# Reordering the first projections, running the first feed-forward in split passes, and moving the last layer's row sums to VectorE

## The reference, cut to what matters

```python
# layer 0, attention: 32 heads of 128, 4 key/value heads, keys from [context, latents]
q = (latents @ Wq).reshape(b, q_len, 4, 8, 128)
k = (hidden_states @ Wk).reshape(b, kv_len, 4, 128)
v = (hidden_states @ Wv).reshape(b, kv_len, 4, 128)
...
# layer 0, feed-forward: a base product and 8 low-rank experts, mixed by a softmax over the batch mean
base = jnp.einsum('bsi,oi->bso', x, W_org)
q = jnp.einsum('bi,ki->bk', x.mean(axis=1), Wq)
coeffs = jax.nn.softmax(jnp.einsum('bk,ek->be', q, lora_keys) / math.sqrt(K), axis=-1)
h = jnp.einsum('bsi,eir->bser', x, lora_down)
delta = jnp.einsum('be,bser,ero->bso', coeffs, h, lora_up)
return base + delta * (SCALE * MULTIPLIER)
...
# layer 3, attention: a product of two fake-quantised matrices, q1 from the norm, q2 from the context
return jnp.matmul(q1, q2)
```

## Time and profile before

| | |
|---|---|
| median of 3 runs | 1441.21 us (1439.42 to 1441.31) |
| the profiled execution, its own time | 1436.33 us |
| its span | 1433.7 us |
| busy share of the span: PE, PEld, DVE, ACT, POOL | 95%, 75%, 65%, 42%, 33% |
| feed-forward 0, its three products (L867, L874, L911) on PE | 16.2, 14.5 and 13.9 us busy |

### The profile page before, as it was taken

The page is one execution under the profiler, slowest core; times in us unless marked ns, Lnnn a source line. Parts: engine busy times, 40 slices in busy tenths (PEclk is TensorE's granted clock), DMA queues, the critical chain, the costliest instruction groups (busy, mean ns, idle before and its releaser), DMA issues.

```text
span 1433.7 us, 21149 instructions
## 1 busy us (share of the span) xinstructions
PE 1359.5 (95%) x8222; PEld 1080.4 (75%) x8227; DVE 927.7 (65%) x1351; ACT 602.6 (42%) x1046; POOL 473.3 (33%) x361
## 2 busy tenths in 40 slices
PE   4999999999999999989999999999989999799986
PEld 3989889988889889874598888888876444377733
DVE  4488778864588688772457775567665576334278
ACT  2444444443344444430144443344425577323252
POOL 4226436371126426512222653217133000324210
PEclk9999999999999999999999999999999699999999
DMA  5111112121012111102111101002004000263000
GB/s 176 52 39 59 56 40 59 36 70 37 16 53 58 53 52 41 34 1 86 44 38 45 33 29 56 23 18 73 1 1 128 1 2 2 91 159 110 1 0 30
DMA packets 54337, 68.18 MB, mean 48 GB/s; under 512 B 26417, under 2 KB 34897, under 8 KB 54241
## 3 DMA queue, kind: packets, MB, share of 16 engines
q1 hardware_dynamic: 54240, 66.84, 15.5%
HBM read 57.13 MB, written 5.37 MB: 44 GB/s over the span
## 4 chain that ended last, share of the span: by engine, by line
PE 85%; DVE 9%; ACT 3%; issue 1%; DMA 1%; POOL 0%; SPq 0%; DVEq 0%; ACTq 0%; POOLq 0%
PE ps L644 13%; PE ps L619 12%; PE ps L595 9%; PE ps L628 9%; PE ps L588 9%; PE ps L580 5%; PE ps L565 5%; PE ps L1508 4%; PE ps L1129 3%; PE ps L1155 3%; PE ps L1521 2%; PE ps L1111 2%; PE ps L1140 1%; PE ps L867 1%; PE ps L874 1%
## 5 line engine op out<-in xcount | busy, mean ns | idle before, releaser
L713 ACT ACTIVATE pT<-ps 128x768 fp32r<-128x768 f32 x192 | 156.0, 812 | 288.6 <-PE ps L628 287.0
L644 PE MATMUL ps<-pT,vv 128*128 128x256 f32 (+1 forms) x1728 | 251.2, 290 | 2.5 <-DVE oT L823 2.5
L619 PEld LDWEIGHTS ps<-kT,qT 128*128 128x128 f32 (+1 forms) x1152 | 201.5, 188 | 43.9 <-DVE qT L768 3.7
L619 PE MATMUL ps<-kT,qT 128*128 128x512 f32 (+3 forms) x1152 | 231.6, 336 | 2.8 <-DVE qT L768 2.8
L816 DVE TENSOR_TENSOR pT<-ps,pT 128x768 fp32r<-128x768 f32 x192 | 183.7, 957 | 77.8 <-ACT pT L713 77.1
L644 PEld LDWEIGHTS ps<-pT,vv 128*128 128x128 f32 (+1 forms) x1728 | 215.1, 180 | 3.1 <-DVE pT L816 2.9
L721 ACT ACTIVATE prob<-ps,rows_and_turned 128x768 f32<-128x768 f32 x192 | 172.3, 897 | 84.9 <-DVE rows_and_turned L804 84.9
L804 DVE TENSOR_REDUCE rows_and_turned<-ps 128x1 f32<-128x768 f32 x192 | 182.7, 951 | 26.1 <-PE ps L619 25.8
L531 POOL TENSOR_TENSOR wo<-raw,one 128x512 fp32r<-128x512 f32 (+1 forms) x48 | 49.9, 1040 | 394.7 <-PE ps L595 394.3
L595 PE MATMUL ps<-wo,oT 128*128 128x512 f32 (+1 forms) x576 | 169.5, 403 | 5.6 <-DVE qT L768 2.6
L628 PE MATMUL ps<-ident,prob 128*128 128x128 f32 x1152 | 157.1, 272 | 0.4 <-DVE pT L816 0.4
(11 more groups left out here) (236 smaller groups left out, 1890.9 us busy)
## 6 DMA issues: line engine op xcount, KB each, us to landing
f2raw<-in_f_w SPq DMA_DIRECT2D x11, 776.0 KB, 5.0
rows_and_turned<-in_m_w SPq DMA_DIRECT2D x11, 768.0 KB, 4.2
raw<-in_l_wq SPq DMA_DIRECT2D x32, 256.0 KB, 2.7
raw<-in_l_wo SPq DMA_DIRECT2D x32, 256.0 KB, 2.6
raw<-in_l_wq SPq DMA_DIRECT2D x16, 192.0 KB, 2.4
raw<-in_l_wo SPq DMA_DIRECT2D x16, 192.0 KB, 2.4
w3gu<-rows_and_turned SPq DMA_DIRECT2D x11, 256.0 KB, 3.1
ctxraw<-in_ctxT SPq DMA_DIRECT2D x2, 1024.0 KB, 7.4
```

What stands on the lines that cost most here:

```text
L619: last = nc.tensor.matmul(sc[:, lo:hi], qT[0:hd, h % 2, qp, r * P:(r + 1) * P], kT[0:hd, kp, b, lo:hi], start=(qp, kp) == PAIRS[0], stop=( ...
L644: last = nc.tensor.matmul(bank(6, 256, hd), vv[:, vp, b * VT + j, group % 2 * hd:(group % 2 + 1) * hd], pT[:, q % 2, pp, j, :], start=(j = ...
L713: nc.scalar.activation(turned_p(m, HI), ps[:, 4:6, 0:S // 2].rearrange("p a (j c) -> p a j c", j=3), ACT.Copy).then_inc(sem("att_pT_hi"), 1)
```

## The change

Three places change.

1. **The start.** `wk` is loaded before the context. The first context half is split in two parts of two k tiles each, on ACT and DVE, and K job 0 starts on the first. Both parts are split ahead of the norm's statistics, and the second half of the context after the turned rows. POOL computes `rstd` behind the split of `wk`, its first stream entry, and goes on to the next weights with no wait for the context, whose raw copy now lies elsewhere. PE's order is K 0, turns, K 2, Q 0, K 1, and K 1 goes to bank 5.
2. **Feed-forward 0.** All three products run as three split passes. POOL splits `worg` in four pieces during heads 22 to 27 of attention 0. `down` and `up` are loaded when the last scores are done, ACT writes their HI parts when the last weighted sums are, and POOL writes their LO parts (one instruction of 128x2048 each), the first of them only when all four norm rows are written (`rows_ready`). DVE splits the turned rows, in between its norm work, and makes the batch sums in two reductions. The small product with the batch mean comes after the base product, `h` is evicted by ACT (HI) and DVE (LO), and the matmuls that spread the coefficients come directly before the last `down_part`. POOL's first split of attention 1's `wv` waits for the small product.
3. **Attention 3.** DVE writes `rowz` instead of ACT, the row sums of a tile come before the turn of the next, the two small ACT instructions of a row no longer wait for each other, and one add and one clamp on DVE change places.

```diff
         self.first = [("K", 0, 0), ("K", 0, 1), ("K", 0, 2), ("Q", 0, 0)]
+        if before is None:
+            self.first = [("K", 0, 0), ("K", 0, 2), ("Q", 0, 0), ("K", 0, 1)]
...
-            sb("kept0", [P, 12, 512], F32, grp)
+            sb("kept0", [P, 31, 512], F32, grp)
             ctxraw = sb("ctxraw", [P, KT, B * CTX], F32, grp)
...
+        CTX_PARTS = ((0, 0, 2), (0, 2, KT), (1, 0, KT))
...
-                if j == 2:
+                if A is A0 and entry in base_after:
...
+                    nc.gpsimd.tensor_tensor(worg_hi[:, k, :], worg[:, k, :], one[:].to_broadcast([P, D]),
+                                            ALU.mult).then_inc(sem("f0_worg_split"), 1)
...
+                if j == (0 if A is A0 else 2):
                     layer_norm()
...
             if A is A0:
-                pe.wait_ge(sem("ctx_split"), 1)
                 job(A.first[0])
                 turn_pe(pe, u)
-                pe.wait_ge(sem("ctx_split"), 2)
+                pe.wait_ge(sem("xT_lo"), RT)
                 job(A.first[1])
+                job(A.first[2])
+                pe.wait_ge(sem("ctx_split"), 3)
+                job(A.first[3])
...
+                    ln_row_variance(v, s, r, sem("att_w"), A.before["w"] + A.place[what])
+                    if r:
+                        ln_row_out(v, s, r - 1)
+                    if r >= 2:
+                        turn_dve(v, 1, [r - 2], "f0_xT_lo")
+                    if r == RT - 1:
+                        ln_row_out(v, s, r)
...
         def mlp0_sp(sp):
-            sp.wait_ge(sem("layer_done"), 1)
+            att_wait(sp, A0, "scores", A0.items)
...
+        def mlp0_weight_lo(g, dst, raw_weights, n):
+
+            g.wait_ge(sem("f0_w_hi"), n)
+            nc.gpsimd.tensor_tensor(dst[:, LO].rearrange("p k n -> p (k n)"),
+                                    raw_weights[:].rearrange("p k n -> p (k n)"),
+                                    dst[:, HI].bitcast(F32).rearrange("p k n -> p (k n)"),
+                                    ALU.subtract).then_inc(sem("f0_w_lo"), 1)
+
         def mlp0_pool(g):
 
+            g.wait_ge(sem("rows_ready"), RT * 2)
+            mlp0_weight_lo(g, downs, down, 1)
...
             def base(r):
+                pe.wait_ge(sem("f0_xT_lo"), r + 1)
                 for k in range(KT):
-                    nc.tensor.matmul(bank(4 + r), xTf[:, k, r * P:(r + 1) * P], worg[:, k, :],
-                                     start=(k == 0), stop=False)
+                    for xp, wp in PAIRS:
+                        nc.tensor.matmul(bank(4 + r), xT[:, xp, k, r * P:(r + 1) * P],
+                                         (worg_hi, worg_lo)[wp][:, k, :], start=(k == 0 and (xp, wp) == PAIRS[0]),
+                                         stop=False)
...
-            def before_output_weights():
-                ln_first_pool(g)
-                g.wait_ge(sem("ctx_split"), 2)
-
-            att_pool(g, A0, before_output_weights)
+            att_pool(g, A0, lambda: ln_first_pool(g))
...
             split_context(0)
+            split_context(1)
             ln_first_dve(v)
-            split_context(1)
             turn_dve(v, 0)
+            split_context(2)
```

More of the change, by code:

```diff
@@ L425, in turn_act, with turn_dve @@
                                      ACT.Copy).then_inc(sem("xT_hi"), 1)
-        def turn_dve(v, u, which=range(RT)):
+        def turn_dve(v, u, which=range(RT), done="xT_lo"):
             for r in which:
@@ L523, in att_pool @@
                     att_wait(g, A, "w_full", A.place["V", h - 2, 5] if h else 0)
+                    if A is A1 and h == 0 and part == 0:
+                        g.wait_ge(sem("f0_small"), 1)
                 elif w == "q":
@@ L562, in job @@
                     for k in range(KT):
+                        if what == ("K", 0, 0) and A is A0 and k % 2 == 0:
+                            pe.wait_ge(sem("ctx_split"), k // 2 + 1)
                         for wp, xp in PAIRS:
@@ L910, in mlp0_pe @@
                         pe.wait_ge(sem("f0_hT"), (k * B + r // 2) + 1)
-                    last = nc.tensor.matmul(bank(4 + r), hT[:, k, r * P:(r + 1) * P], up[:, k, :],
-                                            start=False, stop=(k == KT - 1))
+                    for hp, wp in PAIRS:
+                        last = nc.tensor.matmul(bank(4 + r), hT[:, hp, k, r * P:(r + 1) * P], ups[:, wp, k, :],
+                                                start=False, stop=(k == KT - 1 and (hp, wp) == PAIRS[-1]))
@@ L913, in mlp0_pe, with mlp0_early_act @@
                 last.then_inc(sem("f0_out"), 1)
+        def mlp0_early_act(a):
+            att_wait(a, A0, "pv", A0.pairs)
+            for dst, raw_weights, name in ((downs, down, "f0_down"), (ups, up, "f0_up")):
+                a.wait_ge(sem(name), 16)
+                nc.scalar.activation(dst[:, HI].rearrange("p k n -> p (k n)"),
+                                     raw_weights[:].rearrange("p k n -> p (k n)"),
+                                     ACT.Copy).then_inc(sem("f0_w_hi"), 1)
         def mlp0_act(a):
@@ new lines, in mlp0_act @@
+            for k in range(KT):
+                a.wait_ge(sem("f0_h"), k + 1)
+                for b in range(B):
+                    nc.scalar.activation(hT[:, HI, k, b * 256:(b + 1) * 256], ps[:, k, b * 256:(b + 1) * 256],
+                                         ACT.Copy, scale=spread[:, k, b:b + 1]).then_inc(sem("f0_hT_hi"), 1)
+        def mlp0_dve(v):
+            for b in range(B):
+                if b == 0:
+                    turn_dve(v, 1, [2], "f0_xT_lo")
+                else:
+                    turn_dve(v, 1, [3], "f0_xT_lo")
+                v.wait_ge(sem("f0_xT_lo"), 2 * b + 2)
+                nc.vector.tensor_reduce(msum[:, :, b], xT[:, :, :, b * 256:(b + 1) * 256].bitcast(F32).rearrange(
+                    "p s k n -> p k s n"), AX.XY, ALU.add).then_inc(sem("f0_msum"), 1)
@@ L1724, in att3_row_act @@
             act_seq.inc(nc.scalar.activation(scale, rstd[:, r:r + 1], ACT.Copy, scale=inv[:, 0:1]))
-            act_seq.wait(a)
-            act_seq.inc(nc.scalar.activation(shift, minus_mean, ACT.Identity, scale=scale, bias=sz[:, 1:2]))
+            act_seq.inc(nc.scalar.activation(shift, minus_mean, ACT.Identity, scale=rstd[:, r:r + 1], bias=sz[:, 1:2]))
             act_seq.wait(a)
```

157 lines of the change are left out of this document (95 added, 62 removed).

## The result

The changed kernel takes 1422.97 us (median of 4 runs, 1421.02 to 1428.04); the kernel before took 1440.32 in the four runs beside them. The ratio is 0.9889, 95% interval 0.9863 to 0.9916. The profiled execution took 1423.66 (span 1421.8), 12.7 us under the 1436.33 of before.

A forecast was written before the change was run, and what follows sets the result against it. PE was taken to bound the kernel, with 85% of the chain. Gains of 3.2 (start), 7.0 (feed-forward 0) and 0.2 (attention 3), 10.4 in all, off a median of 1441.2 gave 1430.8 us, range 1425 to 1435.5.

The forecast's parts named there:

- The median of the runs is 4.9 above that execution: Whole kernel: median taken as 4.9 us above the profiled execution, turning 1425.9 into a forecast of 1430.8.
- step 5: Start, clock: K job 2 begins at the low level, costing 1.4 us, bounds 0.4 and 2.1; scores at 32.4.
- Start, 3.2 forecast: Reordered start: first scores at 32.4 instead of 35.66, a gain of 3.2 us with norm rows held by POOL.
- Steps 1 to 4: Start: K job 0 from 8.9 to 13.8, rstd at 14.1, held norm rows 5.7 us, K job 2 at 22.5.
- Feed-forward 0, 7.0 forecast: Feed-forward 0: twelve groups of split passes gain 7.3 us, less a 0.3 stall, giving 7.0.
- 3.43 less 2.82: Feed-forward 0: four float32 matmuls take 3.43 us, twelve split passes 2.82, so 0.61 per group.
- The stall before the last down part: Feed-forward 0: coefficient matmuls directly before the wait for their copy cost 0.3 us, between 0 and 0.6.
- The row's 235 ns: Feed-forward 0: a profile row's time per pass, gain 7.3 us, preferred to the skill page's 216 ns, gain 10.1.
- Attention 3, 0.2 forecast: Attention 3: changed part gains little before DVE takes up mh; 0.2 us, from -0.5 to 1.
- The norm rows not being held: Rival at the start: norm rows unhindered by POOL, scores at 27.8, start gain 7.9, time 1426.1; chance 0.26.
- VectorE did not bound base: Rival in feed-forward 0: two-part sums take twice 2.29, some 3 us lost, gain 7.4, time 1433.8; chance 0.14.
- Slower through the clock: Rival in feed-forward 0: PE's clock stays low, passes 0.41 instead of 0.235, time 1456; chance 0.04.

The follow-up runs named there:

- e7: Changed kernel plus matmuls whose result nobody reads, filling TensorE's waits at the start: median 1419.82 us, ratio to before 0.9870.
- e3: Kernel before with only the feed-forward 0 part of the change: median 1429.90 us, ratio to before 0.9928.
- e1: Kernel before, unchanged, run again against itself: twelve runs from 1431.39 to 1451.21 us.
- e4: Kernel before with only the last layer's part of the change (attention 3): median 1437.09 us, ratio to before 1.0000.
- e10: Changed kernel without the start's part, so the start as before: median 1424.92 us.
- e6: Changed kernel with GpSimd waiting for the four norm rows before splitting the first query weights: ratio to before 0.9864; median 1419.19 us together with e11.
- e11: Repetition of e6, the changed kernel with GpSimd's wait for the norm rows: median 1418.21 us, ratio to before 0.9873.
- e9: e6 with the last layer left as in the kernel before: median 1423.64 us, ratio to before 0.9913.

## Why the prediction was wrong, step by step

**The step that failed is the last one of the sum:** "The median of the runs is 4.9 above that execution". I carried the distance between one profiled execution and three timed runs over to another kernel as if it were a constant. It is not one, because both ends of it move with TensorE's mean clock. Before's 69 runs have a median of 1438.9, the three that I had were 1439.4 to 1441.3, and the profiled one, 1436.33 at clock 0.980, is an ordinary run. The changed kernel's profiled execution is as good as its median, 1423.66 and 1423.70. Without the 4.9 the forecast is 1425.9, 2.2 above that median, and the range moved with it is 1420.1 to 1430.6, which holds the result.

**The forecast gain was too small as well.** The miss of 7.8 us (1430.8 against 1422.97) divides by the medians into 2.3 for the base (1441.2 against 1438.9), 4.8 for the gain (10.4 against 15.2) and 0.7 for the draw of the first four runs. At equal clock the whole change is worth 13.4. To set the forecast beside that, the 1.4 that step 5 took off for the clock goes back: 11.8, so the work was undersized by 1.6. By the slope of the runs 0.001 of clock is 2.9 low us (1435 x 0.001 / 0.5) and 1.08 us of time, so a low us costs about 0.37. The terms:

- *Start, 3.2 forecast, that is 4.6 of work less 1.4 of clock.* At equal clock 5.1 to 5.6 were measured, by the medians 1.2 to 1.6. Steps 1 to 4 stood: key job 0 from 8.94 to 14.35 (forecast 8.9 to 13.8), `rstd` at 14.04 (14.1), norm rows 5.29 (5.7), key job 2 at 21.95 (22.5). Step 5 is the mis-sized term: it gave 1.4 to the clock, with 2.1 as its upper bound, but all twelve passes ran low, 2.7, and the query job behind them lost 0.2 more, so the scores came at 33.0 (32.4), 2.7 earlier than before. The 7 to 10 more low us at 0.37 each are 2.6 to 3.8, and e7, which takes them away, is 3.9 faster by the medians and 0.4 at equal clock.
- *Feed-forward 0, 7.0 forecast, 8.1 measured at equal clock and 9.0 by the medians.* Between the traces the stretch from the turned row to attention 1's keys went from 48.7 to 41.3, 7.4, with 3 us at the low level in both. In the chain from the first base product it is 8.3, where base begins 0.5 later behind the turned row. Twelve passes took 2.76 to 2.80 in base and in the third product (5.51 and 11.19 over 24 and 48), but 2.91 to 3.07 in the down parts. Two groups did not fit the forecast's 3.43 less 2.82: base's first, which was at the low level for 3.4 us before and for 1.7 us here, went from 5.13 to 3.62, and the down parts' four matmuls had taken 3.53 to 3.63. The stall before the last down part was 0.25 (forecast 0.3), and no product waited for a split weight. The row's 235 ns was right for base and the third product; the 216 ns of the Trainium skill ("TensorE: Matmul & The Clock Gate", "Back-to-back issue gap") are not reached here, the 48 passes of `up` take 233 each. About 0.7 more came from attention 0, which is 607.5 us instead of 608.3 in every kernel with the new feed-forward. In e3 against e1 it appears between 494 and 520 us, where a wait of TensorE for VectorE's `qT` of 0.45 is gone; why that wait went I didn't test.
- *Attention 3, 0.2 forecast, 0 measured at equal clock* (-0.3 with e4's 95% spread of about 0.5). In time it brought 1.9 alone (e4), 5.0 in e10 against e3 and 4.4 in e6 and e11 against e9, all by the medians and through a higher mean clock. The forecast had no term for that, and its cause stays open.

**The rivals.** The norm rows not being held was priced at 27.8 for the scores. It was not what happened, but e6 shows the price: 27.1. Held rows are what the forecast, and the rule of the Trainium skill that it named ("GPSIMD Engine Reference", "Key points"), said; the trace agrees, 5.29 against 1.92, and e6 shows the cause. VectorE did not bound base: the two sums took 2.27 and 2.29 with both parts, so the rival's doubling was wrong. Slower through the clock did not happen. The range had no term for the spread of the clock, and before alone covers 20 us; nor are 2.9 us enough to tell two kernels apart by three or four runs each.

**Where the gain lies between the two traces,** 11.9 us of span: start 2.7, attention 0 0.8, feed-forward 0 7.4, layer 1 and the projections of attention 2 -1.9, from there to the last layer 6.0, last layer -3.1. The last three net 1.0. Two of them are code that didn't change, and in all three the low us differ. Read from these two traces alone, attention 2 would have looked like the second largest gain of the change.

## What to carry to other kernels

Before a time is forecast or explained, set the runs' times against their mean granted clock. Here they lay on a line, so the distance of a profile from the median of a few runs was no constant. A comparison at equal clock shows what a change does to the work, and the medians of many runs show what it does to the time. The two can differ: the start is worth 5.1 to 5.6 us by the first and 1.2 to 1.6 by the second.

A low-clock stretch that comes back in every trace of the same code, as the ten us at the start, is part of the price of that code. One that comes and goes between traces of one program, as the 3 and 7 us in before's feed-forward 0, is not; give it a share of the range.

Let GpSimd wait, if it has slack, when a short chain of VectorE instructions on SBUF tensors is what TensorE waits for.

## What the runs showed of the hardware

Key job 0 took 5.41 and 5.46 in the changed kernel and in e6, 0.45 a pass, while its window shows the full granted clock; behind sixteen matmuls of 128x128 it took 3.00 (e7). The window in the changed kernel:

```profile
9.00:14.00 5.00, 5.00 (x12) 1.00 0.87 327
```

So the first passes behind TensorE's idle start were slow though the granted clock doesn't show it. The load of the DMA engines is not the reason: their share was 0.93 in e7's window too.

In these traces VectorE and GpSimd take turns by whole instructions where VectorE works from SBUF to SBUF. In e6 the context split on VectorE, two SBUF tensors of 128x2048, begins at 18.44 while a GpSimd split runs to 19.43, and takes 3.13 instead of 2.28; GpSimd's next, from 19.51, ends 1.17 after it and is recorded as 3.23 instead of 1.27. In e7 the two are recorded as beginning together, at 20.81 and 20.80; the context split took 2.28, and only GpSimd's took longer, 3.44. A split that reads PSUM is not held (four in 2.48 in e6).

In attention 2 the clock falls while TensorE is busy nearly without a gap: 13.71 of 14 us in 1096 to 1110 of the changed kernel are busy. Just before, up to 1096.44, it waited three times, 0.29 each.
